# Splitting the front and back parts of a slot block and interleaving them, in the soft-MoE logits and dispatch stage of an AdaLN layer

## The chip, the cores and the metric

One Trainium2 chip, all eight NeuronCores. The kernel is one launch of the same program on each core. Each core takes one of the eight batch elements of x (2048 tokens by 1024), holds the weights for itself, and exchanges nothing with the others. The metric is the device time of the slowest core, in microseconds (us). Engines: TensorE (PE, with its weight loads shown as PEld), VectorE (DVE), ScalarE (ACT), GpSimd (POOL) and SyncE (SP), which run their own instruction queues and wait for each other by semaphores.

## The reference, cut to what matters

The layer is attention with a window of 7 tokens, followed by a soft mixture-of-experts feed-forward; both are modulated by c and added to x. The changed stage computes the first half of the feed-forward: the logits between normalised tokens and normalised slots, and the dispatch of tokens into slots.

```python
def _L0_ffn_ref(x, gamma_x, gamma_slot, slot_embeds, w1, w2):
    b, s, d = x.shape                       # 8, 2048, 1024
    e, t, _ = slot_embeds.shape             # 8, 512: 4096 slots
    xn = rms_norm(x, gamma_x)
    se = rms_norm(slot_embeds, gamma_slot)
    logits = jnp.einsum('bsd,etd->bset', xn, se)
    dispatch = jax.nn.softmax(logits, axis=1)            # over tokens
    slots = jnp.einsum('bsd,bset->betd', xn, dispatch)
    h = jax.nn.gelu(slots @ w1, approximate=False)
    processed = h @ w2
    combine = jax.nn.softmax(logits.reshape(b, s, e * t), axis=-1)
    out = jnp.einsum('bnd,bsn->bsd', processed.reshape(b, e * t, d), combine)
    return out
```

## The kernel before

The program is written with a small recorder, `Prog`. `P.run` (line 65 records what it emits) and `P.runf` append an instruction to the list of one engine, the first with a drain ahead of it on VectorE and ScalarE; `P.wait` appends a wait for a semaphore value, unless that engine has already waited for at least that value; `P.dma` (line 98) appends a DMA to GpSimd's queue ("g") or SyncE's. So the order in which the Python code calls these is the order on each engine, and nothing is reordered later. The three semaphores t, v and s count finished work of TensorE, VectorE and ScalarE.

The stages follow each other with fences at the borders: p0 and p1 (modulation, attention, normalised tokens in two layouts, xn_tm with tokens on partitions and xn_fm with features on partitions), p2 (the changed one, from about 1137 to 2236 us), p3 (slots times w1, gelu), p4 (times w2), p5 (combine, output).

Stage p2 walks over SC = 32 blocks of 128 slots. For each block `sc`:

- `p2_front(sc)`: GpSimd issues the load of setm (the slot embeddings, 128 x 1024) for block sc+1. TensorE transposes block sc into the PSUM tile pSe (line 965), VectorE multiplies it by gpre into sefs (973). TensorE multiplies sefs with xn_fm into four PSUM tiles pL, 32 matmuls of 128x512 (983): the logits of 128 slots by 2048 tokens. VectorE takes the maximum over the tokens of each pL (993), the maximum of the four (995) and the bias of the exponential (997). ScalarE computes the exponentials of the four pL into ach (1008), with their sums, and then copies the four pL, scaled, into lch (1017). VectorE adds the sums and takes the reciprocal (1023, 1025). GpSimd issues eight DMAs that spill lch to memory (L_sp).
- `p2_back(sc)`: TensorE transposes ach into the PSUM tile pAt, in two sets of eight (1048); after each set VectorE copies pAt into atm (1057). pAt is one bank, so the second set waits for the first copy. TensorE multiplies atm with xn_tm into two PSUM tiles pDs, 32 matmuls of 128x512 (1066). VectorE scales pDs by the reciprocal into slsm (1079) and sets a mark on colD (1083). TensorE transposes slsm into pSe (1092), VectorE copies it into slots_fm (1099).

ach, lch, atm, slsm and setm have two buffers each, by the parity of sc. pL, pAt, pDs and pSe have one set each, and take all eight banks of PSUM together. The next front's matmuls into pL wait for ScalarE's copies of the block before (`lev_l`).

The main loop runs the front of a block and then the back of the block before:

```python
            for sc in range(SC):
                p2_front(sc)
                if sc >= 1:
                    p2_back(sc - 1)
            p2_back(SC - 1)
```

Of the kernel before, what the change touches and what calls it, by code (L numbers as in the profile page):

```python
# [23 lines left out]
SC = S // 128  # L24
# [102 lines left out]
def build(stop_after=None, debug=False):  # L127
# [50 lines left out]
    with g:  # L178
# [730 lines left out]
        with ExitStack() as es2:  # L909
# [21 lines left out]
            lmk_hist = [None] * SC  # L931
# [21 lines left out]
            def p2_front(sc):  # L953
                buf = sc % 2
# [24 lines left out]
                lmk = None  # L979
                for j in range(DJ):  # L980
                    for nb in range(4):
                        lmk = P.run("tensor", lambda e, buf=buf, j=j, nb=nb:
                                    e.matmul(  # L983
                            pL[nb][:, 0:512],
                            se_fs[buf][:, j * 128:(j + 1) * 128],
                            xn_fm[:, j * N + nb * 512:j * N + (nb + 1) * 512],
                            start=(j == 0), stop=(j == DJ - 1)),
                            "t" if (j == DJ - 1 and nb == 3) else None)
                lmk_hist[sc] = lmk
                p = 4 * (sc % 2)  # L990
                P.wait("vector", "t", lmk)
                for nb in range(4):
# [36 lines left out]
                                   l_ch[buf][:, nb8 * 256:(nb8 + 1) * 256])  # L1029
                             for nb8 in range(NBL)]  # L1030

            def p2_back(sc):
                buf = sc % 2
                p = 4 * (sc % 2)
                P.wait("tensor", "s", aemk_l[sc])
                if sc >= 1:
                    P.wait("tensor", "v", disv[sc - 1])
                atev = None
                for pk in range(2):
                    mk = None  # L1040
                    if pk == 1:
                        P.wait("tensor", "v", atev)
                    elif sc >= 1:
                        P.wait("tensor", "v", atev_prev[0])
                    for t8 in range(8):
                        nt = pk * 8 + t8
                        mk = P.run("tensor", lambda e, buf=buf, nt=nt, t8=t8:
                                   e.transpose(  # L1048
                            pAt[:, t8 * 128:(t8 + 1) * 128],
                            a_ch[buf][:, nt * 128:(nt + 1) * 128], ident_bf[:]),  # L1050
                            "t" if t8 == 7 else None)
                    if pk == 1:
                        atr_hist[sc] = mk
                    P.wait("vector", "t", mk)
                    if sc >= 2:
                        P.wait("vector", "t", dis_m[sc - 2])
                    atev = P.runf("vector", lambda e, buf=buf, pk=pk: e.tensor_copy(  # L1057
                        a_tm[buf][:, pk * 1024:(pk + 1) * 1024], pAt[:, 0:1024]),
                        "v")
                atev_prev[0] = atev  # L1060
                P.wait("tensor", "v", atev)
                dmk = None
                for nt in range(NT):
                    for half in range(2):
                        dmk = P.run("tensor", lambda e, buf=buf, nt=nt, half=half:
                                    e.matmul(  # L1066
                            pDs[half][:, 0:512],
                            a_tm[buf][:, nt * 128:(nt + 1) * 128],
                            xn_tm[:, nt * D + half * 512:nt * D + half * 512 + 512],
                            start=(nt == 0), stop=(nt == NT - 1)),  # L1070
                            "t" if (nt == NT - 1 and half == 1) else None)
                dis_m[sc] = dmk
                P.wait("vector", "t", dmk)
                if sc >= 2:
                    P.wait("vector", "t", stm_hist[sc - 2])
                P.waitm("vector", ("v", rdcol[sc]))
                for half in range(2):
                    P.runf("vector", lambda e, buf=buf, half=half, p=p:
                           e.tensor_scalar(  # L1079
                        sl_sm[buf][:, half * 512:(half + 1) * 512],  # L1080
                        pDs[half][:, 0:512], colC[:, 10 + p:11 + p], None,
                        ALU.mult))
                dis_l = P.runf("vector", lambda e: e.memset(colD[:, 3:4], 0.0), "v")
                disv[sc] = dis_l
                P.wait("tensor", "v", dis_l)
                if sc + 1 < SC:
                    P.wait("tensor", "v", sfold_m[sc + 1])
                elif sc >= 1:
                    P.wait("tensor", "v", sfm_m[sc - 1])
                mk = None  # L1090
                for j in range(DJ):
                    mk = P.run("tensor", lambda e, buf=buf, j=j: e.transpose(
                        pSe[:, j * 128:(j + 1) * 128],
                        sl_sm[buf][:, j * 128:(j + 1) * 128], ident_bf[:]),
                        "t" if j == DJ - 1 else None)
                P.wait("vector", "t", mk)
                sfm_last = None
                for jj in range(DJ):
                    sfm_last = P.runf("vector", lambda e, jj=jj, sc=sc: e.tensor_copy(
                        slots_fm[:, jj * S + sc * 128:jj * S + sc * 128 + 128],  # L1100
                        pSe[:, jj * 128:(jj + 1) * 128]),
                        "v" if jj == DJ - 1 else None)
                stm_hist[sc] = mk
                sfm_m[sc] = sfm_last

            atev_prev = [None]
            for sc in range(SC):
                p2_front(sc)
                if sc >= 1:
                    p2_back(sc - 1)  # L1110
            p2_back(SC - 1)

            P.emit("p2")
            if debug:
# [360 lines left out]
```

How the kernel before makes its waits and increments, by code:

```python
    def wait(self, eng, sem, val):  # L57
        if val is None or val <= 0:
            return
        w = self.waited[eng]
        if w.get(sem, -1) >= val:
            return
        w[sem] = val
        h = self.sems[sem]
        self.ops[eng].append(lambda e: e.wait_ge(h, val))
# [6 lines left out]
    def run(self, eng, fn, sem=None, k=1, chain=True):  # L72
        if chain and eng in ("vector", "scalar"):
            self.ops[eng].append(lambda e: e.drain())
        if sem is None:
            self.ops[eng].append(fn)
            return None
        self.counts[sem] += k
        mark = self.counts[sem]
        h = self.sems[sem]
        self.ops[eng].append(lambda e: fn(e).then_inc(h, k))
        return mark
# [4 lines left out]
    def dma(self, q, dst, src):  # L87
        eng = self.QENG[q]
        i = self.qidx[q]
        self.qidx[q] += 1
        key = q + str(i % self.QDEPTH[q])
        prior = self.counts[key]
        if prior > 0:
            self.wait(eng, key, prior)
        self.counts[key] += 16
        val = self.counts[key]
        h = self.sems[key]
        self.ops[eng].append(lambda e: e.dma_start(dst, src).then_inc(h, 16))
        return (key, val)
```

## Time and profile before

| | us |
|---|---|
| median of two runs | 3782.16 |
| the two runs | 3755.82 and 3808.51 |
| profiled execution | 3759.67 |
| its span, slowest core (core 2) | 3758.1 |
| spans of the eight cores | 3743.2 to 3758.1 |
| mean granted clock of TensorE, core 2 and core 6 | 0.826 and 0.797 |
| stage p2 on core 2 | about 1137 to 2236 |

In the profiled execution the cores are within 0.4% of each other, and the trace that is read below is that of core 2. A row of the page gives the busy time of a group of instructions, their number and the mean time of one; the timeline merges instructions of one kind that follow each other, with their start, how long they took together, and in brackets the idle time of the engine before them and what ended it. The end of a row of matmuls is modelled: the next row on TensorE can start a little before it. The granted clock is 1.00 at 2.4 GHz and 0.50 at 1.2 GHz; a stretch with both levels shows a value between.

### The profile page before, as it was taken

Reading aid. Unit: us, or ns where it says so; the run is one execution under the profiler, and the core shown is the slowest. Engines: PE = TensorE matmul, PEld = TensorE weight load, DVE = VectorE, ACT = ScalarE, POOL = GpSimd, SP = SyncE. Lnnn points to the kernel's source line nnn. Section 1 sums busy time; section 2 is a strip of 40 time slices with the busy share of each in tenths; the row PEclk is TensorE's granted clock in tenths of the full one; section 3 lists DMA queues with packets and bytes.
Section 4 is the critical chain, followed back from the end, with each engine's and each line's share of the span. In section 5 each row is a group of like instructions: output and inputs, shape, how many; then the busy total and the mean of one; then the engine's idle time right before and its main releaser. Section 6 shows DMA issues by size and latency. Waiting matters only on the chain. (4 is left out here: it accounts for less than half of the span.)

```text
span 3758.1 us, 33154 instructions; the slowest of 8 cores (3743.2 to 3758.1 us)
## 1 busy us (share of the span) xinstructions
PE 2563.8 (68%) x11776; PEld 1183.1 (31%) x11776; DVE 964.7 (26%) x1998; ACT 626.4 (17%) x1213; POOL 548.8 (15%) x1021
## 2 busy tenths in 40 slices
PE   5317656665645565656565646888876999968888
PEld 0203222222212222222222222333332444435554
DVE  0443333332772222222222220000004000023332
ACT  0110212111221111111111111222210000023332
POOL 5000000000001111111111113555551000000000
PEclk9999666665767777788778777999986999979888
DMA  9140121102221111111111124222227232243440
GB/s 145 37 81 12 45 40 41 39 23 51 90 79 48 28 42 42 42 29 42 42 42 28 42 50 101 68 65 65 67 75 138 68 90 68 67 128 107 135 135 34
DMA packets 138944, 241.78 MB, mean 64 GB/s; under 512 B 34967, under 2 KB 80279, under 8 KB 137758
## 3 DMA queue, kind: packets, MB, share of 16 engines
q0 software_dynamic: 78864, 138.49, 16.1%
q1 hardware_dynamic: 59918, 101.16, 9.1%
q8 instruction: 98, 1.61, 0.2%
q14 instruction: 64, 0.52, 0.1%
HBM read 201.85 MB, written 83.89 MB: 76 GB/s over the span
## 5 line engine op out<-in xcount | busy, mean ns | idle before, releaser
L1152 PE MATMUL pH<-slots_fm,w_bf 128*128 128x512 bf16 x2048 | 458.8, 384 | 98.5 <-DMA h_sp<-hbuf 54.2
L1239 PE MATMUL pP<-w_bf,hblk 128*128 128x512 bf16 x2048 | 459.1, 386 | 32.1 <-DVE w_bf L1217 18.2
L983 PE MATMUL pL<-xn_fm,sefs 128*128 128x512 bf16 x1024 | 294.5, 459 | 58.7 <-DVE sefs L973 49.0
L98 POOL DMA_DIRECT2D h_sp<-hbuf x512 | 273.0, 541 | 284.3 <-ACT hbuf L1163 273.8
L1152 PEld LDWEIGHTS pH<-slots_fm,w_bf 128*128 128x128 bf16 x2048 | 197.9, 98 | 359.0 <-issue 135.8
L1066 PE MATMUL pDs<-xn_tm,atm 128*128 128x512 bf16 x1024 | 288.4, 451 | 30.2 <-DVE atm L1057 30.2
L1239 PEld LDWEIGHTS pP<-w_bf,hblk 128*128 128x128 bf16 x2048 | 199.6, 98 | 292.7 <-issue 59.1
L98 POOL DMA_DIRECT2D L_sp<-lch x256 | 136.9, 542 | 921.8 <-ACT lch L1017 919.1
L1008 ACT ACTIVATE ach<-pL,colC,rscale_all 128x512 bf16<-128x512 f32 x128 | 97.8, 773 | 877.3 <-DVE colC L997 877.3
L1379 PE MATMUL pO<-proc_sm,w_smb 128*128 128x512 bf16 x1024 | 226.0, 382 | 0.9 <-DVE w_smb L1364 0.9
L1048 PE MATMUL pAt<-ident_bf_s,ach 128*128 128x128 bf16 x512 | 51.5, 262 | 240.3 <-DVE atm L1057 240.3
L1163 ACT ACTIVATE hbuf<-pH 128x512 bf16<-128x512 f32 x256 | 132.2, 602 | 367.0 <-PE pH L1152 367.0
L983 PEld LDWEIGHTS pL<-xn_fm,sefs 128*128 128x128 bf16 x1024 | 114.3, 114 | 228.9 <-issue 155.5
L1066 PEld LDWEIGHTS pDs<-xn_tm,atm 128*128 128x128 bf16 x1024 | 112.3, 112 | 198.9 <-issue 122.6
L993 DVE TENSOR_REDUCE colA<-pL 128x1 f32<-128x512 f32 x128 | 79.5, 684 | 306.8 <-PE pL L983 296.3
L1253 DVE CAST proc_sm<-pP 128x512 bf16<-128x512 f32 x64 | 41.2, 686 | 389.9 <-PE pP L1239 389.9
L1379 PEld LDWEIGHTS pO<-proc_sm,w_smb 128*128 128x128 bf16 x1024 | 100.7, 98 | 120.2 <-issue 4.3
L1199 DVE COPY row_c<-pQ 1x512 f32<-1x512 f32 x1 | 0.7, 678 | 521.1 <-PE pQ L1193 521.1
L1079 DVE TENSOR_SCALAR slsm<-pDs,colC 128x512 bf16<-128x512 f32 x64 | 45.1, 746 | 299.2 <-PE pDs L1066 299.2
L1048 PEld LDWEIGHTS pAt<-ident_bf_s,ach 128*128 128x128 bf16 x512 | 41.4, 117 | 252.2 <-issue 244.9
L809 PE MATMUL pp<-w_out_bf,attn_cat 128*128 128x512 bf16 x256 | 89.0, 517 | 23.2 <-DVE colD L834 18.7
L1313 PE MATMUL pT<-ident_f_s,lblk 128*128 128x128 f32 x512 | 87.8, 352 | 20.8 <-DMA lblk<-L_sp 20.8
(184 smaller groups left out, 2499.6 us busy)
## 6 DMA issues: line engine op xcount, KB each, us to landing
L_sp<-lch POOLq DMA_DIRECT2D x256, 128.0 KB, 2.2
h_sp<-hbuf POOLq DMA_DIRECT2D x512, 64.0 KB, 1.8
lblk<-L_sp SPq DMA_DIRECT2D x8, 4096.0 KB, 17.1
se_st<-slot_embeds POOLq DMA_DIRECT2D x32, 512.0 KB, 3.6
wsl<-wmod POOLq DMA_DIRECT2D x96, 128.0 KB, 8.1
xst<-x SPq DMA_DIRECT2D x16, 512.0 KB, 3.9
xrs<-x SPq DMA_DIRECT2D x16, 512.0 KB, 4.2
x_sp<-x2b POOLq DMA_DIRECT2D x16, 512.0 KB, 5.0
```

Of the source, the lines that this page charges most:

```text
L98: self.ops[eng].append(lambda e: e.dma_start(dst, src).then_inc(h, 16))
L809: P.run("tensor", lambda e, i=i, j=j, half=half: e.matmul(pp[2 + 2 * (i % 2) + half][:, 0:512], attn_cat[:, j * N + i * 128:j * N + i * 12 ...
L983: e.matmul(pL[nb][:, 0:512], se_fs[buf][:, j * 128:(j + 1) * 128], xn_fm[:, j * N + nb * 512:j * N + (nb + 1) * 512], start=(j == 0), stop ...
L993: P.runf("vector", lambda e, nb=nb, p=p: e.reduce_max(colA[:, 8 + p + nb:9 + p + nb], pL[nb][:, 0:512], AX.X))
L1008: e.activation(a_ch[buf][:, nb * 512:(nb + 1) * 512], pL[nb][:, 0:512], AF.Exp, bias=colC[:, 9 + p:10 + p], scale=rscale_all[:, sc:sc + 1] ...
L1048: e.transpose(pAt[:, t8 * 128:(t8 + 1) * 128], a_ch[buf][:, nt * 128:(nt + 1) * 128], ident_bf[:]),
L1066: e.matmul(pDs[half][:, 0:512], a_tm[buf][:, nt * 128:(nt + 1) * 128], xn_tm[:, nt * D + half * 512:nt * D + half * 512 + 512], start=(nt ...
L1152: e.matmul(pH[pbase + q][:, 0:512], w1_bf[:, j * HID + hc * 128:j * HID + (hc + 1) * 128], slots_fm[:, j * S + hf * 2048 + q * 512: j * S ...
L1163: e.activation(h_buf[hc % 2][:, q * 512:(q + 1) * 512], pH[pbase + q][:, 0:512], AF.Gelu),
L1239: e.matmul(pP[2 * (st % 2) + half][:, 0:512], h_blk[blk % 2][:, hc * HBW + st * 128: hc * HBW + (st + 1) * 128], w2_bf[:, hc * D + half * ...
L1313: e.transpose(pT[t16 // 4][:, (t16 % 4) * 128:(t16 % 4) * 128 + 128], l_blk[nb % 2][:, sc * NBW + ti * 128: sc * NBW + (ti + 1) * 128], id ...
L1379: e.matmul(pO[half][:, 0:512], w_smb[:, sc * 128:(sc + 1) * 128], proc_sm[:, sc * D + half * 512: sc * D + half * 512 + 512], start=(sc == ...
```

## The change

The front and the back part are each cut in two, and the four pieces are called in another order. No instruction is added, removed or changed.

- The front is cut after the matmuls into pL. What follows them (maximum, bias, exponentials, copies into lch, sum, reciprocal, spills) is now `p2_fB(sc)`.
- The back is cut after the copies of pAt. `p2_backT1(sc)` is the transposes and copies, `p2_backT2(sc)` the rest, from the matmuls into pDs on.
- The loop calls front(sc), backT1(sc-1), fB(sc), backT2(sc-1).

```diff
@@ -987,6 +987,10 @@
                             start=(j == 0), stop=(j == DJ - 1)),
                             "t" if (j == DJ - 1 and nb == 3) else None)
                 lmk_hist[sc] = lmk
+
+            def p2_fB(sc):
+                buf = sc % 2
+                lmk = lmk_hist[sc]
                 p = 4 * (sc % 2)
                 P.wait("vector", "t", lmk)
                 for nb in range(4):
@@ -1029,9 +1033,8 @@
                                    l_ch[buf][:, nb8 * 256:(nb8 + 1) * 256])
                              for nb8 in range(NBL)]
 
-            def p2_back(sc):
+            def p2_backT1(sc):
                 buf = sc % 2
-                p = 4 * (sc % 2)
                 P.wait("tensor", "s", aemk_l[sc])
                 if sc >= 1:
                     P.wait("tensor", "v", disv[sc - 1])
@@ -1058,6 +1061,11 @@
                         a_tm[buf][:, pk * 1024:(pk + 1) * 1024], pAt[:, 0:1024]),
                         "v")
                 atev_prev[0] = atev
+
+            def p2_backT2(sc):
+                buf = sc % 2
+                p = 4 * (sc % 2)
+                atev = atev_prev[0]
                 P.wait("tensor", "v", atev)
                 dmk = None
                 for nt in range(NT):
@@ -1107,8 +1115,12 @@
             for sc in range(SC):
                 p2_front(sc)
                 if sc >= 1:
-                    p2_back(sc - 1)
-            p2_back(SC - 1)
+                    p2_backT1(sc - 1)
+                p2_fB(sc)
+                if sc >= 1:
+                    p2_backT2(sc - 1)
+            p2_backT1(SC - 1)
+            p2_backT2(SC - 1)
 
             P.emit("p2")
             if debug:
```

## Rows read from the trace of the kernel before

**Rows 1.** The page: busy time of each engine, and the slices.

```profile
PE 2563.8 (68%) x11776; PEld 1183.1 (31%) x11776; DVE 964.7 (26%) x1998; ACT 626.4 (17%) x1213; POOL 548.8 (15%) x1021
...
PE   5317656665645565656565646888876999968888
```

**Rows 2.** A stretch of stage p2: us, busy per engine, clock, DMA share, GB/s.

```profile
1300.00:1400.00 100.00, 59.97 (x284) 27.07 (x283) 24.84 (x66) 16.39 (x36) 14.46 (x27) 0.76 0.15 40
```

**Rows 3.** Waits of stage p2: engine line <- releaser, us, times, longest.

```profile
PE pAt L1048 <- DVE atm L1057: 240.3, 32, 8.0
...
PE pSe L1092 <- DVE colD L1083: 56.1, 32, 2.1
```

**Rows 4.** Timeline of a block: start us, us, engine, operation, idle before.

```profile
1605.39 8.62 PE L983 MATMUL pL<-xn_fm,sefs 128*128 128x512 bf16 x32 [1.58 <-DVE sefs L973]
1613.85 0.61 PE L1048 MATMUL pAt<-ident_bf_s,ach 128*128 128x128 bf16 x8
1614.12 2.48 DVE L993 TENSOR_REDUCE colA<-pL 128x1 f32<-128x512 f32 x4 [8.98 <-PE pL L983]
...
1620.75 2.43 ACT L1017 ACTIVATE lch<-pL,rscale_all 128x512 f32<-128x512 f32 x4
1620.96 0.16 DVE L1023 TENSOR_REDUCE colC<-colB 128x1 f32<-128x4 f32 x1 [3.84 <-ACT ach L1008]
...
1621.29 0.69 DVE L1057 COPY atm<-pAt 128x1024 bf16<-128x1024 bf16 x1
1622.13 1.01 PE L1048 MATMUL pAt<-ident_bf_s,ach 128*128 128x128 bf16 x8 [7.67 <-DVE atm L1057]
1623.25 0.69 DVE L1057 COPY atm<-pAt 128x1024 bf16<-128x1024 bf16 x1 [1.26 <-PE pAt L1048]
1623.77 4.28 POOL L98 DMA_DIRECT2D L_sp<-lch  x8 [29.31 <-ACT lch L1017]
1624.09 9.50 PE L1066 MATMUL pDs<-xn_tm,atm 128*128 128x512 bf16 x32 [0.94 <-DVE atm L1057]
1633.77 1.41 DVE L1079 TENSOR_SCALAR slsm<-pDs,colC 128x512 bf16<-128x512 f32 x2 [9.82 <-PE pDs L1066]
...
1635.33 0.61 PE L1092 MATMUL pSe<-ident_bf_s,slsm 128*128 128x128 bf16 x8 [1.74 <-DVE colD L1083]
1636.04 1.14 DVE L1099 COPY slots_fm<-pSe 128x128 bf16<-128x128 bf16 x8 [0.86 <-PE pSe L1092]
...
1639.52 1.01 PE L983 MATMUL pL<-xn_fm,sefs 128*128 128x512 bf16 x2 [1.58 <-DVE sefs L973]
```

**Rows 5.** Pieces of the block from 1571.26, columns as in rows 2.

```profile
1571.30:1574.60 3.30, 3.30 (x9) 1.16 (x10) 0.00 (x0) 0.00 (x0) 0.00 (x0) 0.53 0.00 0
1574.60:1579.90 5.30, 5.30 (x29) 2.45 (x28) 0.00 (x0) 0.00 (x0) 0.00 (x0) 1.00 0.00 0
1580.40:1588.00 7.60, 0.00 (x0) 0.03 (x1) 3.39 (x9) 4.42 (x11) 0.00 (x0) 0.78 0.00 0
1588.00:1595.00 7.00, 6.06 (x21) 2.52 (x22) 0.69 (x1) 1.05 (x2) 4.82 (x9) 0.51 0.45 152
1595.00:1599.40 4.40, 4.40 (x21) 1.84 (x19) 0.00 (x0) 0.00 (x0) 0.00 (x0) 1.00 0.42 61
```

**Rows 6.** Timeline of TensorE at the stage's end: the last block's back.

```profile
2221.22 0.61 PE L1048 MATMUL pAt<-ident_bf_s,ach 128*128 128x128 bf16 x8 [1.55 <-DVE atm L1057]
2222.77 8.75 PE L1066 MATMUL pDs<-xn_tm,atm 128*128 128x512 bf16 x32 [0.94 <-DVE atm L1057]
```

**Rows 7.** A dense stretch later, core 2 and core 6, columns as in rows 2.

```profile
2900.00:3000.00 100.00, 100.00 (x465) 45.30 (x463) 9.02 (x14) 0.00 (x0) 0.00 (x0) 1.00 0.28 76
...
2900.00:3000.00 100.00, 99.47 (x455) 45.33 (x464) 9.02 (x14) 0.00 (x0) 0.00 (x0) 1.00 0.27 76
```

**Rows 8.** Timeline of TensorE: pL in an earlier block.

```profile
1330.06 9.74 PE L983 MATMUL pL<-xn_fm,sefs 128*128 128x512 bf16 x32 [1.58 <-DVE sefs L973]
```

**Rows 9.** A DMA issue of stage p2: KB each, median us from issue to landing.

```profile
setm<-slot_embeds POOLq DMA_DIRECT2D x32, 256.0 KB, 4.0
```

## The prediction

> **What bounds the kernel now.** The page comes first. TensorE is the engine with most work, 68% of the span, and no other passes 26% [rows 1]. But the slices show that it is not busy evenly: digits of 5 and 6 from about a third to three fifths of the span, against 9 later on. The chain that ended last is of no help here, as it reaches back only into the last stage. So I cut the span by stage: in a 100 us stretch of stage p2 TensorE is busy 60 us, VectorE 25, ScalarE 16, GpSimd 14, DMA 15%, at a granted clock of 0.76 [rows 2]. Nobody is full: the stage is bound by engines that wait in turn. The waits of this stage say where: of all that TensorE waits for, 240.3 us is the transposes into pAt waiting for VectorE's copy out of pAt (atm), 32 times, at most 8.0; the others are 56.1 us and less [rows 3]. (ScalarE's and GpSimd's waits, longer in total, are those of engines with little to do.)
>
> The timeline of one block of 128 slots shows why [rows 4]. TensorE starts pL at 1605.39 and the next pL at 1639.52: a block takes 34.13 us. After pL it puts eight transposes into pAt (1613.85), and they sit there: VectorE has first the maxima over pL (1614.12) and the bias, then it waits 3.84 us for ScalarE's four exponentials, then come sum (1620.96) and reciprocal, and it copies pAt only at 1621.29. TensorE's second eight transposes start at 1622.13, after 7.67 us idle. The copied block is one back (sc-1): it needs nothing of what VectorE did in between.
>
> The granted clock in the pieces of the block just before this one (pL from 1571.26): 0.53 in the first 3.3 us of pL, then 1.00; it falls in the 7.6 us stall (0.78 there), is 0.51 from the second transposes to 1595.0, some 5 us into pDs, then 1.00 again, and has fallen when the next pL starts (0.53) [rows 5]. Full is 2.4 GHz, half 1.2. So each stall is paid twice, once idle and once in the slow start of the work behind it.
>
> **The block before, in steps** (start to start, all from [rows 4]): pL 8.46 (1605.39 to 1613.85); first transposes to second 8.28; second to pDs 1.96; pDs to slsm 9.68 (1624.09 to 1633.77); slsm to its transposes 1.56; from there over the transposes of setm to the next pL 4.19 (1635.33 to 1639.52). Sum 34.13.
>
> **The change, part by part.** No instruction is added or taken out, only the order on each engine. On TensorE nothing moves, since the part of the front that is split off holds no TensorE work: its order is as before. On ScalarE and GpSimd the order stays too: exponentials, copies to lch, eight spills and the setm load stand in one file as before. On VectorE the two atm copies of block sc-1 now come ahead of the maximum, bias, sum and reciprocal of block sc.
>
> 1. *The stall between the two sets of transposes.* VectorE is idle when pL ends. From the start of eight transposes to the start of the VectorE work on them it takes 0.71 us (1635.33 to 1636.04), and from an atm copy's start to the next transposes 0.84 (1621.29 to 1622.13). Together 1.55 in place of 8.28: 6.73 saved.
> 2. *Second transposes to pDs.* They took 1.01 us at the low clock and 0.61 at full. The last block of the stage, which has no front ahead of it, shows the after-change order at full clock: transposes at 2221.22, pDs at 2222.77, 1.55 in place of 1.96 [rows 6]. 0.41 saved.
> 3. *pDs itself.* If the clock is still full when it starts: TensorE in a dense stage does 465 matmuls of this size in 100 us, 0.215 each [rows 7], so 32 take 6.88, and slsm follows 0.35 later (the row's 9.50 ends at 1633.59, 0.18 before slsm, and holds the last matmul's pipeline, some 0.17 by pL, which is 8.62 long while its successor starts after 8.46), 7.23 in place of 9.68: 2.45 saved. If not, nothing is saved, or what the last block shows: its pDs took 8.75 although only gaps of 1.55 and 0.94 stood ahead of it [rows 6]. Bounds 0 and 2.45. I take 2.45 for the common block: the 7.67 us stall, in which the clock fell, is gone, and idle pieces of 0.9 are short beside 8.5 us of pL. (In the last block no matmuls of pL stand ahead of the transposes, as they do in all others.)
> 4. *pL.* Nothing ahead of it changes, so it starts slow as now. But how much of it is slow differs now by where it starts: 8.46 in this block (8.62 in its row), about 9.6 in blocks earlier in the stage (9.74 in the row) [rows 8]. With a shorter block the start will drift against the clock's steps; I take the middle, 9.0, that is 0.55 lost against this block.
> 5. *VectorE's moved chain, now beside pDs.* From the maximum's start to the place of the next VectorE work it took 7.17 (1614.12 to 1621.29), with 3.84 of it waiting for ScalarE, and this chain must be over before slsm, which stands behind it on VectorE. The maximum now starts after the second copy, 0.69 from that copy's start, so slsm can start 0.69 + 7.17 = 7.86 after it; TensorE's side gives 0.83 (1623.25 to 1624.09, rounded) + 7.23 = 8.07. The chain costs nothing, but with only 0.2 us to spare: pDs is its cover. Whatever makes the chain longer by more than that shows at once, one for one, 31 times.
> 6. *Who waits for the later chain.* The next pL needs ScalarE's copies out of pL. They end 9.06 after the maximum's start (1620.75 + 2.43 - 1614.12), and slsm starts 8.07 - 0.69 = 7.38 after it, so 1.7 before they end; pL starts 5.75 after slsm (1633.77 to 1639.52): cover 4.0 us. The spills start behind these copies; GpSimd issues eight in 4.28 us [rows 4] and setm behind them, which lands 4.0 us after its issue [rows 9]. The setm issued then is for the block after next, so it has over 20 us left. Per block GpSimd issues under 5 us of 25. The DMA share of 0.15 becomes 0.2, where a later, dense stage runs at 0.28 [rows 2, 7]. Nothing.
>
> New block: 9.0 + 1.55 + 1.55 + 7.23 + 1.56 + 4.19 = 25.1 us, against 34.13: 9.05 saved. It is saved each time a back part follows a front's, 31 times of 32 (the last back stands alone as before): 31 x 9.05 = 280 us. The next stage begins with fences and weight loads of the core's own, which only start earlier. The profiled execution took 3759.7 us, so 3480. (The two runs shown are 3755.8 and 3808.5, whose median is 22 above the profiled one; I forecast for an execution like the profiled one.) The measurement can tell a change from none at about 2%, 75 us.
>
> **A rule that speaks against it.** On the core of the rows and on core 6, which has the lowest mean clock of the eight (0.797), 465 and 455 recorded matmuls fall into 100 us of the dense stage at granted clock 1.00, with all eight cores at the same work [rows 7]. The Trainium skill (TensorE: Matmul & The Clock Gate, Seeing it yourself) warns that a die with three cores in dense matmuls is held at 13/16 of the clock. By that rule the 64 large matmuls of a block would take some 0.05 us more each, an estimate from that page's ratio, so the block 28.3 and the kernel about 3580, which is rival D below at a milder price; the trace does not agree in its densest stage, which has no such level.
>
> **The rivals.**
> A. As above, 3480, own range 3460 to 3500 (pL between 8.46 and 9.6).
> B. The stall goes, pDs stays slow. The last block's 8.75 speaks for it, the full clock at pL's end against it. Or VectorE's chain grows by 2 us because ScalarE reads pL while TensorE writes pDs, with the same result. Block: 34.13 - 6.73 - 0.41 = 27.0; 31 x 7.14 = 221: 3538.
> C. pL too starts at full clock in most blocks, as less idle time stands in a block. Then 6.9 for pL, block 23.0, 31 x 11.1 = 345: 3415. Against it: the two idle pieces and few transposes ahead of pL, over which the clock falls today, are not touched.
> D. All eight cores' denser work keeps the clock in pDs below full: between A's 3480 and, at half clock, 13.76 for pDs (twice 6.88), block 32.0, 31 x 2.1 = 66 saved, 3694, within 2%. The dense stage [rows 7] speaks against it.
> E. The other side: the same, for both pDs and pL. Twice 13.76 gives 36.7 a block, 31 x 2.6 = 80 more: 3840. It decides once the clock takes more than 9.05 us from a block. Only a stage with less busy TensorE than the dense one would have to be clocked lower than it is now.
> F. VectorE's order isn't what decides, since another wait holds pAt: the second transposes also wait for marks of earlier work. But all those marks (disv, dis_m, atev_prev) are of the block before and done by pL's end; the idle of TensorE ends 0.15 after the copy. 3760.
>
> **How the numbers follow.** A 0.62, B 0.20, C 0.09, D 0.05, E 0.02, F 0.02. Over 2% faster: A, B, C and, of D, the 0.03 that lie below 3685, 0.94. Within 2%: 0.04. Slower: 0.02. The range: A and B hold 0.82; down to 3440 (a block of 23.8, part of the way to C), up to 3560 (B's 3538, and the 22 us that a median can stand above the profiled execution).
>
> **What would show it.** In the timeline of after: the second transposes into pAt 1.55 after the first; the atm copies ahead of the maximum; pDs about 6.9 to 7.1 long; slsm's start released by pDs rather than by the reciprocal (right if TensorE's side is the longer); pL still 8.5 to 9.6; blocks of 24.5 to 25.7. The wait of pAt for atm drops from 240.3 us to about 30. TensorE's granted clock over the stage rises from 0.76 towards 0.85. Blocks of 27 with pDs at 9 would say B, of 23 C. The prediction is wrong in its mechanism if the idle before slsm is ended by ScalarE's work, or if the next pL waits for lch.

## The result, and the profile after

The changed kernel takes 3480.84 us in the median (3759.31 before in the same series); the ratio is 0.9237, with a 95% interval of 0.9202 to 0.9272. (Some executions of either kernel are in a slower state, with one die at a lower clock; this ratio, and those below, compare the means of the fast executions alone, which is why it is not the quotient of the two medians.) That is 7.6% faster, and the forecast was 3480 (3440 to 3560). The profiled execution has a span of 3477.9 us on its slowest core, 280.2 less than the 3758.1 before; the cores lie between 3463.6 and 3477.9. The rows below are of core 7. Line numbers have moved by up to 12: atm is L1060, pDs L1074, slsm L1087.

The page of the kernel after, with the busy time of the engines and the slices:

```profile
PE 2491.9 (72%) x11776; PEld 1159.9 (33%) x11776; DVE 964.1 (28%) x1998; ACT 626.0 (18%) x1213; POOL 547.1 (16%) x1021
...
PE   5318566565654677777777488888759999868888
```

The instruction counts are those of [rows 1], and VectorE, ScalarE and GpSimd are busy as long as before. TensorE's busy time is 72 us less, though it does the same work: that is the higher clock in the changed stage (0.88 against 0.76). The mean granted clock of a whole core doesn't show it (0.817 on core 7 here, 0.826 on core 2 before), nor does it say much of a core otherwise: the values of 0.82 and 0.86 on the cores of this execution differ by the first 300 us, where the trace says 0.57 on core 7 and 1.00 on core 0, with the same busy time (118.6 and 118.2). So it is with core 6 of the kernel before, which the prediction names for its lowest mean. The stretch of 5 and 6 has become one of 7, and is shorter.

Three waits of TensorE and VectorE in the stage after (us in total, times, longest), to be held against [rows 3]:

```profile
PE pSe L1100 <- DVE colD L1091: 55.9, 32, 1.8
...
PE pAt L1051 <- DVE atm L1060: 30.8, 32, 1.5
...
DVE slsm L1087 <- PE pDs L1074: 16.7, 30, 9.1
```

The wait of the transposes for the copy out of pAt has gone from 240.3 us to 30.8. The other one shown has stayed (56.1 before). And slsm waits for pDs 16.7 us in all, 9.1 of it in the last block, where before VectorE stood idle 9.8 us ahead of slsm in a block [rows 4]: the chain of maxima, exponentials and reciprocal now fills that time.

One block in the timeline after:

```profile
1608.77 9.84 PE L983 MATMUL pL<-xn_fm,sefs 128*128 128x512 bf16 x32 [1.58 <-DVE sefs L973]
...
1618.45 0.61 PE L1051 MATMUL pAt<-ident_bf_s,ach 128*128 128x128 bf16 x8
1619.17 0.69 DVE L1060 COPY atm<-pAt 128x1024 bf16<-128x1024 bf16 x1 [10.65 <-PE pAt L1051]
1620.01 0.61 PE L1051 MATMUL pAt<-ident_bf_s,ach 128*128 128x128 bf16 x8 [0.94 <-DVE atm L1060]
1620.72 0.69 DVE L1060 COPY atm<-pAt 128x1024 bf16<-128x1024 bf16 x1 [0.86 <-PE pAt L1051]
1621.33 2.48 DVE L997 TENSOR_REDUCE colA<-pL 128x1 f32<-128x512 f32 x4
1621.56 7.07 PE L1074 MATMUL pDs<-xn_tm,atm 128*128 128x512 bf16 x32 [0.94 <-DVE atm L1060]
...
1627.95 2.43 ACT L1021 ACTIVATE lch<-pL,rscale_all 128x512 f32<-128x512 f32 x4
1628.16 0.16 DVE L1027 TENSOR_REDUCE colC<-colB 128x1 f32<-128x4 f32 x1 [3.84 <-ACT ach L1012]
1628.39 0.16 DVE L1029 RECIPROCAL colC<-colC 128x1 f32<-128x1 f32 x1
1628.80 1.41 DVE L1087 TENSOR_SCALAR slsm<-pDs,colC 128x512 bf16<-128x512 f32 x2 [0.24 <-PE pDs L1074]
...
1635.12 8.63 PE L983 MATMUL pL<-xn_fm,sefs 128*128 128x512 bf16 x32 [1.74 <-DVE sefs L973]
```

In the steps of the prediction: pL 9.68 (1608.77 to 1618.45), first to second transposes 1.56, second to pDs 1.55, pDs to slsm 7.24, slsm to the next pL 6.32. pDs takes 7.07, with TensorE at full clock from its start; it was 9.50. VectorE's chain starts with the maxima 0.23 us ahead of pDs and ends under it, and 0.24 us is left between its end and slsm.

The granted clock in the pieces of this block (us from the span's start, length, busy time of PE, PEld, DVE, ACT and POOL, then the clock), against [rows 5]:

```profile
1608.80:1612.50 3.70, 3.70 (x9) 1.25 (x10) 0.00 (x0) 0.00 (x0) 1.22 (x3) 0.50 0.65 164
...
1618.50:1621.50 3.00, 1.17 (x17) 0.85 (x15) 1.47 (x3) 0.00 (x0) 0.00 (x0) 1.00 0.00 0
1621.60:1628.60 7.00, 7.00 (x32) 2.99 (x32) 2.89 (x8) 3.69 (x10) 0.00 (x0) 1.00 0.00 0
1628.70:1635.00 6.30, 1.62 (x16) 1.24 (x16) 3.79 (x12) 1.68 (x3) 4.03 (x8) 0.72 0.34 116
```

Where the block before had two falls of the clock, one in the stall and one between pDs and pL, this one has the second alone.

Blocks come in three lengths, about 24.3, 24.7 and 26.3 us; a long one is followed by one or two short ones. pL starts also at:

```profile
1584.47 8.36 PE L983 MATMUL pL<-xn_fm,sefs 128*128 128x512 bf16 x32 [1.61 <-DVE sefs L973]
...
1659.77 9.94 PE L983 MATMUL pL<-xn_fm,sefs 128*128 128x512 bf16 x32 [1.61 <-DVE sefs L973]
```

With the two starts in the block above, that is 24.30, 26.35 and 24.65 us, 25.1 in the mean. In the long ones pL takes more (9.84), and the transposes of setm 1.01 in place of 0.61. Over all blocks from the second start of pL to the last, the mean is 25.27 on core 7 (25.24 to 25.34 on the others), and 34.25 on core 2 of the kernel before. 31 x 8.98 = 278 of the 280 us.

The 8.98 us by steps, in the means over the same blocks: first transposes to second 6.75, second to pDs 0.40, pDs to slsm 1.93 (9.18 before, 7.25 after), pL 0.05 (9.02 and 8.97), and 0.15 lost between slsm and the next pL. In the block of [rows 4] pDs took 9.50 and pL 8.62. In 14 of the 30 blocks of that core it was the other way, as in the one of [rows 8]:

```profile
1349.88 8.38 PE L1066 MATMUL pDs<-xn_tm,atm 128*128 128x512 bf16 x32 [0.94 <-DVE atm L1057]
```

There pL takes 9.74, and the block is 34.13 long all the same.

### The profile page after: what moved, and what is told of

It reads as the page before. It is cut to its first block and busy times, and to the rows that moved or that the text cites. A ratio compares the mean times of both kernels' runs of the same rounds, so it can differ in the third digit from the quotient of the medians.

```text
span 3477.9 us, 33123 instructions; the slowest of 8 cores (3463.6 to 3477.9 us)
## 1 busy us (share of the span) xinstructions
PE 2491.9 (72%) x11776; PEld 1159.9 (33%) x11776; DVE 964.1 (28%) x1998; ACT 626.0 (18%) x1213; POOL 547.1 (16%) x1021
## 5 line engine op out<-in xcount | busy, mean ns | idle before, releaser
L1074 PE MATMUL pDs<-xn_tm,atm 128*128 128x512 bf16 x1024 | 227.9, 381 | 30.2 <-DVE atm L1060 30.2
L1074 PEld LDWEIGHTS pDs<-xn_tm,atm 128*128 128x128 bf16 x1024 | 98.2, 98 | 149.7 <-issue 37.3
L1060 DVE COPY atm<-pAt 128x1024 bf16<-128x1024 bf16 x64 | 44.3, 692 | 338.1 <-PE pAt L1051 338.1
L1340 ACT ACTIVATE l_tmb<-pT 128x512 f32<-128x512 f32 x128 | 69.9, 605 | 182.5 <-PE pT L1325 182.3
L1346 DVE TENSOR_REDUCE colA<-l_tmb 128x1 f32<-128x4096 f32 x16 | 70.7, 4420 | 106.8 <-ACT l_tmb L1340 106.8
```

What stands on the lines that cost most here:

```text
L1074: e.matmul(pDs[half][:, 0:512], a_tm[buf][:, nt * 128:(nt + 1) * 128], xn_tm[:, nt * D + half * 512:nt * D + half * 512 + 512], start=(nt ...
L1340: e.activation(l_tmb[:, stg * 2048 + q * 512: stg * 2048 + (q + 1) * 512], pT[q][:, 0:512], AF.Copy), "s")
L1346: P.runf("vector", lambda e, p=p: e.reduce_max(colA[:, p:p + 1], l_tmb[:], AX.X))
```

## The experiments

All were timed beside the kernel before on the same chip. Theory 1 is the prediction's: the stall cost its idle time and the slow clock behind it, and the moved chain is covered by pDs with 0.2 us to spare.

### The clock's share by itself: the stall filled, not removed

```diff
# in p2_back of the kernel before, in each block but the last
                     if pk == 1:
+                        for r in range(34):
+                            P.run("tensor", lambda e, r=r: e.matmul(
+                                pDs[r % 2][:, 0:512], ident_bf[:],
+                                xn_tm[:, 0:512], start=True, stop=True))
                         P.wait("tensor", "v", atev)
```

> The kernel before, with its order untouched; in each block but the last TensorE does 34 extra matmuls of 128x512 into pDs between the two sets of transposes, that is in the stall of 7.7 us (34 x 0.215 = 7.3 us). Their results are overwritten by the real matmuls, which start anew. The stall stays, only the idleness in it goes. Theory 1 (the stall costs twice: idle time, and the slow clock behind it): granted clock 1.00 at pDs, pDs 7.1 long in place of 9.5, second transposes 0.61 in place of 1.01, 2.8 us off the block of 34.2 at most, some of it given back in a longer slow start of pL, so a block of 31.4 to 32.2 and the kernel 65 to 85 us faster than before: about 3680 (ratio 0.98). Rival 1 (pDs was slow for another reason, say ScalarE's and VectorE's use of PSUM beside it, and only the stall itself counted): pDs stays at 9 or more, block 34.1, ratio 1.00. The maxima start as before in both.

Measured: ratio 0.9827 (0.9766 to 0.9888), span 3693.0 us; blocks 31.85 us in the mean (34.25 before). The timeline of TensorE in this kernel (L1044 is the filling, L1053 the transposes into pAt, L1071 pDs):

```profile
1589.90 0.61 PE L1053 MATMUL pAt<-ident_bf_s,ach 128*128 128x128 bf16 x8
1590.35 7.50 PE L1044 MATMUL pDs<-xn_tm,ident_bf_s 128*128 128x512 bf16 x34
1598.18 0.61 PE L1053 MATMUL pAt<-ident_bf_s,ach 128*128 128x128 bf16 x8 [0.33 <-DVE atm L1062]
1599.73 7.07 PE L1071 MATMUL pDs<-xn_tm,atm 128*128 128x512 bf16 x32 [0.94 <-DVE atm L1062]
```

The stall is as long as it was (8.28 from first transposes to second), and yet pDs takes 7.07 and the second transposes 0.61. The kernel does more work on its busiest engine and is faster, by less than 2% but clear of noise. Rival 1 falls: pDs was slow because of the clock alone. This is 2.4 us a block, so of the 9.0 that the change brought a quarter is clock and three quarters the stall itself. The Trainium skill (TensorE: Matmul & The Clock Gate, HAM oscillation) describes a loop whose wait throttles the engine anew in each turn, so that the start of the next work is slow each time; this run agrees with it, with 9.50 against 7.07 us for the same 32 matmuls.

### Not quite filled

The same with 28 matmuls in place of 34.

> As the run that fills the stall of the kernel before with extra matmuls, but 28 in place of 34: 6.0 us of the 7.7 us stall filled, 1.6 left idle ahead of the second transposes. If the gain of a filled stall goes with the filled share, 28/34 of that run's 2.3 us a block are to be had: block 32.2, ratio 0.985. If it is the clock alone that counts, all or nothing: either the clock holds, block 32, or it falls over the 1.6 us and the 0.9 us behind them and pDs starts slow (8 us or more), then blocks near 34.1 and a ratio of 1.00, although TensorE was idle for 6 us less in each block. I expect the second.

Measured: ratio 1.0011 (0.9976 to 1.0046), span 3768.4; blocks 34.1 from the fourth on. In the timeline a late block, and then the second one of the stage:

```profile
1609.66 6.21 PE L1044 MATMUL pDs<-xn_tm,ident_bf_s 128*128 128x512 bf16 x28
1617.49 0.61 PE L1053 MATMUL pAt<-ident_bf_s,ach 128*128 128x128 bf16 x8 [1.63 <-DVE atm L1062]
1619.04 8.62 PE L1071 MATMUL pDs<-xn_tm,atm 128*128 128x512 bf16 x32 [0.94 <-DVE atm L1062]
```

```profile
1209.26 0.61 PE L1053 MATMUL pAt<-ident_bf_s,ach 128*128 128x128 bf16 x8 [1.63 <-DVE atm L1062]
1210.81 7.07 PE L1071 MATMUL pDs<-xn_tm,atm 128*128 128x512 bf16 x32 [0.94 <-DVE atm L1062]
```

All or nothing, as expected, and here nearly always nothing. TensorE was idle 6 us less in each block and the time is the same to 0.1%. In 29 of the 31 filled blocks of this core (core 3) pDs starts slow, after idle pieces of 1.63 and 0.94 us with eight transposes between them. But these pieces alone do not decide it: in the second block they are the same, pDs takes 7.07 (on seven of the eight cores), and the block is 31.15 long, like those of the filled stall. What sets it apart was not found. With 0.33 and 0.94 (the filled stall), and with 0.94 and 0.94 (the changed kernel), the clock holds in each of the 31 blocks that follow a front, on all eight cores.

### Half of the change: one copy ahead of the chain

```diff
# on VectorE: first copy of pAt, then maxima .. reciprocal, then the second copy
     for pk in range(2):
         ...
+        if pk == 1 and sc + 1 < SC:
+            p2_fB(sc + 1)
         P.wait("vector", "t", mk)
```

> Half of the change: on VectorE only the first copy out of pAt comes ahead of maximum, bias, sum and reciprocal of the next block; the second copy stays behind them. TensorE's order is that of the other two kernels. Theory 1: the stall isn't halved but moves from ahead of the second transposes to behind them: first copy 0.7 us after the first transposes start, second transposes at 1.55, the maxima at 1.4, the second copy 7.2 after that, pDs 0.8 later, so 9.4 us from first transposes to pDs against 10.2 before and 3.1 after. pDs again starts at the slow clock. Block 33.3 to 34.2: kernel 3730 to 3760, ratio 0.99 to 1.00. Rival 2 (each copy that is moved brings its share): half of the gain, block near 29.7, about 3620, ratio 0.96.

Measured: ratio 0.9966 (0.9946 to 0.9987), span 3756.1; blocks 34.0 to 34.1. The timeline:

```profile
1611.21 0.61 PE L1051 MATMUL pAt<-ident_bf_s,ach 128*128 128x128 bf16 x8
1611.92 0.69 DVE L1063 COPY atm<-pAt 128x1024 bf16<-128x1024 bf16 x1 [9.44 <-PE pAt L1051]
1612.53 2.47 DVE L997 TENSOR_REDUCE colA<-pL 128x1 f32<-128x512 f32 x4
1612.76 0.61 PE L1051 MATMUL pAt<-ident_bf_s,ach 128*128 128x128 bf16 x8 [0.94 <-DVE atm L1063]
...
1619.69 0.69 DVE L1063 COPY atm<-pAt 128x1024 bf16<-128x1024 bf16 x1
1620.53 9.96 PE L1077 MATMUL pDs<-xn_tm,atm 128*128 128x512 bf16 x31 [7.16 <-DVE atm L1063]
```

The stall has moved from ahead of the second transposes (7.67) to behind them (7.16), and pDs starts slow as before. Rival 2 falls: there is no half of this gain. 0.9 us less from first transposes to pDs (9.32 against 10.24) brought only 0.2 a block. In this block pDs takes 9.96 against 9.50, and the transposes of setm 1.01 against 0.61.

### The cover of the moved chain: one and three maxima more

```diff
# in p2_fB of the changed kernel; K = 1 and K = 3
                 P.wait("vector", "t", lmk)
+                for nb in range(K):
+                    P.runf("vector", lambda e, nb=nb: e.reduce_max(
+                        colB[:, nb:nb + 1], pL[nb][:, 0:512], AX.X))
                 for nb in range(4):
```

> The changed kernel with VectorE's chain beside pDs one maximum longer: one extra maximum over pL (0.62 us, written to a column that nobody reads) ahead of the four. Theory 1 (the chain lies under pDs with 0.2 us to spare): slsm is no longer released by pDs but by the chain, 0.4 us later; 31 x 0.4 = 13 us slower, ratio to the changed kernel about 1.003 to 1.006, kernel 3490 to 3502. The waits of slsm for pDs vanish. Rival 3 (the cover is large, or TensorE's clock absorbs it): same time within 3 us as the changed kernel.

> As the run with one extra maximum, with three (1.86 us). Theory 1, straight: 1.86 - 0.2 = 1.66 us a block later, 31 x 1.66 = 51 us, 3532. Theory 1 with the clock: the idle piece of TensorE after pDs grows by 1.66, so the slow start of pL should be longer or the slow stretch start earlier, in every block; then blocks of 27.3 and 3543. Rival 3 (cover of several us): 3480 to 3490.

Measured with one: ratio to the kernel before 0.9299 (0.9261 to 0.9337), span 3499.0. This interval overlaps that of the changed kernel, so what the one maximum costs is read from the blocks: 25.67 in the mean against 25.27, 0.4 more for 0.6 of work. Measured with three: 0.9422 (0.9378 to 0.9466), span 3547.3; blocks 27.3, 2.05 more for 1.8 of work. VectorE's waits in the run with one more:

```profile
DVE slsm L1090 <- PE pDs L1077: 8.8, 1, 8.8
```

In the changed kernel this wait occurs 30 times; here only in the last block. Rival 3 falls: from the start of pDs to slsm it now takes 7.61 us in place of 7.25, and 8.80 with three maxima, 0.60 for each of the two added last. So the first one cost 0.36, and the cover was 0.24, as the row of slsm says. Of the two readings for three maxima the one with the clock is right: the step to slsm is 1.55 longer, the block 2.05. The timeline of TensorE (L1103: slsm's transposes) shows what came on top:

```profile
1510.98 1.01 PE L1103 MATMUL pSe<-ident_bf_s,slsm 128*128 128x128 bf16 x8 [3.30 <-DVE colD L1094]
1513.38 1.01 PE L965 MATMUL pSe<-ident_bf_s,setm 128*128 128x128 bf16 x8 [1.39 <-DVE slots_fm L1110]
```

TensorE's idle piece behind pDs has grown from 1.74 to 3.30, the clock falls in it, and both sets of transposes now take 1.01 in most blocks. In the changed kernel those of slsm always take 0.61, and those of setm 1.01 only in the long blocks. pL is not longer (8.89 to the next transposes, 8.97 in the changed kernel). So the one who waits longer pays again in the clock.

### What is left of the clock: the idle pieces filled (rival C)

```diff
# in the changed kernel: TensorE, transposes of the identity that nobody reads
+ p2_fill(pSe, 12)   # ahead of each wait for an atm copy
+ p2_fill(pAt, 26)   # ahead of the wait for slsm
+ p2_fill(pAt, 20)   # behind slsm's transposes
+ p2_fill(pAt, 22)   # ahead of the wait for sefs
```

> The changed kernel, with extra 128x128 transposes of the identity on TensorE in each of its idle pieces: 12 and 12 around the second transposes (into pSe), 26 after pDs, 20 and 22 around the transposes of setm (into pAt); what they write is overwritten before it is read. No other engine's work changes. Rival C's case: if the slow start of pL is what the idle pieces cost, pL takes 6.9 from start to the next transposes in place of 8.2 to 9.7, the granted clock is 1.00 through the stage, blocks are 22.7 to 23.0 in place of 25.3, and the kernel 70 to 80 us faster than the changed one: ratio to the kernel before 0.90 to 0.91. If the slow start of pL is not from the idle pieces, or the extra work delays what is behind it, the block stays at 25.3 or more: ratio 0.924 or more.

Measured: ratio 0.9088 (0.9066 to 0.9110), span 3417.1, 61 us less than the changed kernel where 70 to 80 were expected; blocks 23.01, but for the first one. The granted clock over 500 us of the stage is 1.00 (0.88 in the changed kernel), and pL takes 7.07:

```profile
1300.00:1800.00 500.00, 467.81 (x4086) 287.85 (x4084) 179.57 (x479) 114.64 (x252) 105.80 (x198) 1.00 0.23 59
```

So the low clock in pL and in setm's transposes, 25.27 - 23.01 = 2.26 us a block, was indeed the price of idle pieces. The run fills those around the second transposes too; but over these the clock held without filling (1.00 in the pieces of the block above), which leaves the ones between pDs and pL. Rival C of the prediction had the right price (block 23.0) and was rightly held unlikely for the change alone, which leaves those pieces.

### A version that beats both: nothing between pDs and the next pL

The steps show 5.8 us from slsm to the next pL in which TensorE does 16 transposes. Their order can be changed too: setm's transposes for the next block inside pDs, slsm's a block later between the two sets into pAt, with VectorE's part in the 3.84 us in which it waited for ScalarE. The new loop, cut to what matters:

```diff
+            for sc in range(SC):
+                p2_pL(sc)                        # at once behind pDs(sc-2)
+                p2_T1(sc - 1, mid=p2_slT(sc - 2))
+                p2_max(sc); p2_fB1(sc)           # maxima, bias, exponentials, lch
+                p2_slcopy(sc - 2)
+                p2_pDs(sc - 1, 0, 10)            # 20 of 32 matmuls
+                p2_seT(sc + 1)                   # transposes of setm, and sefs
+                p2_pDs(sc - 1, 10, NT)
+                p2_fB2(sc); p2_sl(sc - 1)        # sum, reciprocal; slsm
```

> A further reordering on the ground of the chain of steps: the transposes of setm for the next block stand inside pDs (after 20 of its 32 matmuls), slsm's transposes a block later, between the two sets of transposes into pAt, and VectorE's work on both in the time in which it waited for ScalarE. So nothing stands between pDs and the next pL but ScalarE's copies out of pL. By the steps of the rows: pL 6.9 at full clock; first transposes, copy, second transposes, copy 2.3; maxima to the end of the copies into lch 9.1 + 0.7: block 19.0, bound by ScalarE's copies (pL waits for lch, some 1.2 us). 31 x 6.3 = 195 us less than the changed kernel: 3285, ratio to the kernel before 0.873. If the chain through ScalarE is longer, or the clock falls in the remaining pieces of 1 us, blocks of 20 to 22: ratio 0.88 to 0.90.

Measured: ratio 0.8770 (0.8732 to 0.8808), span 3298.4. Two starts of pL:

```profile
1503.97 7.07 PE L983 MATMUL pL<-xn_fm,sefs 128*128 128x512 bf16 x32 [1.45 <-ACT lch L1053]
1522.94 7.07 PE L983 MATMUL pL<-xn_fm,sefs 128*128 128x512 bf16 x32 [1.45 <-ACT lch L1053]
```

A block of 18.97 (19.0 forecast; the kernel was expected at 3285), pL at full clock, and bound as expected by ScalarE's copies into lch, for which pL waits 1.45.

The next version takes that wait away: pL bank by bank, three maxima while pL runs (the diff is cut to the order of the loops).

```diff
-                for j in range(DJ):
-                    for nb in range(4):
+                for nb in range(4):
+                    P.wait("tensor", "s", lev_l[sc - 1][nb])
+                    for j in range(DJ):
```

> As the run with pL at once, and pL computed bank by bank (eight matmuls for one bank of 512 tokens, then the next) in place of all four banks side by side, with a mark and a wait for each bank: VectorE takes three of the four maxima while pL still runs, and pL may start into a bank as soon as ScalarE has copied that one. The chain from the copies of pAt to the end of lch is 1.9 us shorter, and pL starts 1.8 us before that end: TensorE is then the bound, with 15.1 us of work and some 2.2 us of waits for the pAt copies: block 17.3, 31 x 8 = 248 us less than the changed kernel, 3235, ratio to the kernel before 0.860. If bank order costs TensorE something (its 32 weight loads are the same number), pL shows it: over 7.1 us.

Measured: ratio 0.8622 (0.8593 to 0.8652), span 3245.0. Its timeline, and 100 us of the stage:

```profile
1500.66 4.48 PE L1109 MATMUL pDs<-xn_tm,atm 128*128 128x512 bf16 x19 [0.95 <-DVE atm L1095]
...
1508.01 7.07 PE L981 MATMUL pL<-xn_fm,sefs 128*128 128x512 bf16 x31
...
1516.47 0.61 PE L1086 MATMUL pAt<-ident_bf_s,ach 128*128 128x128 bf16 x8 [0.50 <-DVE atm L1095]
...
1518.02 2.32 PE L1109 MATMUL pDs<-xn_tm,atm 128*128 128x512 bf16 x10 [0.94 <-DVE atm L1095]
```

```profile
1300.00:1400.00 100.00, 90.66 (x542) 46.31 (x551) 48.62 (x129) 29.26 (x65) 28.85 (x54) 1.00 0.30 80
```

A block is 17.36 (17.3 forecast), pL starts without a wait, TensorE is busy 91% of these 100 us, at a granted clock of 1.00, and so are the other seven cores (90.6 to 91.4). This version is the best of all: 13.8% faster than the kernel before, where the change is 7.6% faster. What remains in a block is 15.7 us of TensorE's work (90.66% of 17.36) and the two waits for the copies out of pAt, 0.50 and 0.94.

## Why the prediction was right

The terms of its sum, against the block in the timeline after.

1. **The stall**: 1.55 forecast from first transposes to second, 1.56 measured. The wait in total: about 30 forecast, 30.8 measured.
2. **Second transposes to pDs**: 1.55 and 1.55.
3. **pDs to slsm**: 7.23 forecast, 7.24 measured. Of the two bounds (0 and 2.45 saved) the upper one was chosen, on the ground that the stall in which the clock fell was gone. The filled stall shows that ground to be right: the clock is all that made pDs slow. The 2.45 itself holds against the block of [rows 4] only; against the mean of the old blocks it is 1.93. Rival B, which kept pDs slow, is out but was closer than its reason said. Its witness was the last block, with gaps of 1.55 and 0.94. In the changed kernel that block is slow again on five of the eight cores (8.82 on core 7), and at full clock on three (7.07 on core 1), with the same gaps. The prediction set the witness aside because no pL stands ahead of it. The run with 28 matmuls shows that a first gap of about that length can do it even behind dense work (1.63 and 0.94: slow in most blocks), and the common block of the changed kernel has 0.94 there.
4. **pL**: 9.0 in the middle of 8.46 and 9.6. The blocks have 8.36, 9.84, 8.63 and 9.94 in the rows after, less 0.16 of pipeline each: 9.0 in the mean, and 8.97 over the stage. The drift from block to block was foreseen, the regular alternation was not. That pL would lose 0.55 against the block of [rows 4] is true, but in the mean the old blocks had 9.02, so it lost nothing; this is the same half microsecond that pDs did not save.
5. **The cover**: 0.2 us forecast, 0.24 in the row of slsm, and confirmed by the run with one maximum more (0.36 later to slsm for 0.60 of work). The sentence that a longer chain shows "one for one" holds for the start of slsm but not for the block: three maxima put slsm 1.55 us later and made the block 2.05 longer, through the clock.
6. **Who waits for the later chain**: pL of a block never waits for lch but in the first block (9.6 us once, as before).
7. **slsm to the next pL**: 5.75 forecast, as before; 6.32 in the block shown and 5.93 in the mean, since in the long blocks the clock falls ahead of setm's transposes (1.01 in place of 0.61). This step was the one that the prediction left at its old length, and it makes up the 0.17 us that the new block is longer than forecast.

Two small errors cancelled, some 5 us each over the stage; that the forecast of 3480 meets the profiled execution (3479.46) to a microsecond is luck to that extent. The new block was put at 25.1 and is 25.27 in the mean over the stage; the old one at 34.13 and is 34.25, since two blocks are longer than the others (36.40 and 35.08). The difference, 9.05 forecast, is 8.98. TensorE's clock over the stage came to 0.88 where "towards 0.85" was written.

Rivals D and E, a clock kept down by eight denser cores, did not come up: even the last version, with TensorE 91% busy on each of the eight cores, has a granted clock of 1.00 there on all of them. F fell with the wait.

## What to carry to other kernels

Read the order on each engine, not only the dependences: a copy that another engine needs at once stood here behind 7 us of work that nobody needed yet, and moving it needed neither instruction nor buffer. Price a stall of TensorE with the slow start of what follows it, and expect all or nothing there: most of the stall filled, or one of the two copies moved, gave 0.3% or less; the whole of it filled gave 1.7%, and the whole of it removed 7.6%. And after such a move, look at what the moved work is covered by, here 0.2 us of pDs, because the next small addition will be paid in full, and more.

## What was not expected of the hardware

Very different changes left the length of a block at 34.1 us. The block before, the one with 6 us of idleness filled, and the one with one copy moved (0.9 us off its steps) all have it, within 0.2; and 27.3 for the block with three more maxima is nearly as steady (27.3 to 27.4 in about half of the blocks, 26.7 to 27.8 in the others). What was saved in one place was lost at the low clock in another. The kernel before does this by itself: its blocks have either pL 8.62 and pDs 9.50 [rows 4] or pL 9.74 and pDs 8.38, 18.12 together both times. With one copy moved pDs took 9.96 and setm's transposes 1.01; with the 28 matmuls it was pL 9.81 and pDs 8.62. While TensorE's clock fell and rose within a block, a gain of a few tenths of a microsecond could thus vanish in the clock, and only when a fall was avoided altogether did the time drop. The Trainium skill has a passage that fits (TensorE: Matmul & The Clock Gate, A second HAM failure mode): short idle pieces between groups of matmuls suffice to throttle the engine again and again. The runs agree: here pieces of 1.63 and 0.94 us did it in most blocks, and pieces of 0.94 and 0.94 in none of those that follow a front. Why the length settles just there was not tried.
